# One loop over all rounds of a graph-layer kernel, with the second sums one step behind and three separate PSUM banks

## The reference, cut to what matters

```
agg = segment_sum(edge_attr, dst, 6250)        # 200000 edges x 128, dst sorted ascending
h   = relu(concat([x, agg, u[0]]) @ W1 + b1)   # 6250 x 320 @ 320 x 128
out = layernorm(x + h @ W2 + b2)               # 6250 x 128, all float32
```

## Time and profile before

| | |
|---|---|
| median of 3 runs | 278.43 us (277.78 to 278.43) |
| the profiled execution, its own time | 278.17 us |
| its span, first to last instruction | 276.3 us |
| busy: TensorE matmul, weight load | 214.3 us, 169.8 us |
| busy: VectorE, ScalarE, GpSimd | 167.3, 51.2, 41.5 us |
| moved by DMA | 110.06 MB, mean 398 GB/s |
| mean granted TensorE clock | 0.963 |

### The profile page before, as it was taken

One profiled execution on the slowest core, in us unless ns is written; L12 is line 12 of the kernel. 1 busy time (PEld: TensorE's weight loads), 2 busy tenths in 40 slices (PEclk: granted clock), 3 DMA queues, 4 the chain that ended last, 5 costly groups with the idle time before them and its releaser, 6 DMA issues.

```text
span 276.3 us, 15282 instructions
## 1 busy us (share of the span) xinstructions
PE 214.3 (78%) x6759; PEld 169.8 (61%) x6759; DVE 167.3 (61%) x426; ACT 51.2 (19%) x100; POOL 41.5 (15%) x49
## 2 busy tenths in 40 slices
PE   0998698786786796696877789895698897867872
PEld 0886577655665665575555668674577675655751
DVE  7833483774674665655773426959928768464542
ACT  0511122211211220220210211322022212121210
POOL 6400020210310300400400200300303002030020
PEclk9999999999999999999996679999899999999997
DMA  7999999999999999999999999999999999999995
GB/s 249 385 388 401 400 399 401 403 399 402 401 400 403 401 400 402 402 400 413 418 409 412 418 414 417 418 411 421 412 419 418 411 423 412 410 420 412 417 402 188
DMA packets 30911, 110.06 MB, mean 398 GB/s; under 512 B 2136, under 2 KB 3502, under 8 KB 30894
## 3 DMA queue, kind: packets, MB, share of 16 engines
q1 hardware_dynamic: 27508, 105.83, 96.1%
q10 hardware_dynamic: 3386, 4.00, 4.1%
HBM read 106.63 MB, written 3.20 MB: 397 GB/s over the span
## 4 chain that ended last, share of the span: by engine, by line
PE 62%; issue 15%; DMA 12%; DVE 6%; POOL 1%; ACT 1%; DVEq 0%; POOLq 0%; ACTq 0%
PE rows_ps L823 33%; PE cols_ps L835 15%; DMA slots<-in_edge_attr 12%; PE hid_ps L867 4%; PE hid_ps L849 3%; PE hid_ps L858 3%; PE hid_ps L843 2%; ACT rows L426 1%; DVE first_of_pair L551 1%; POOL rstd L390 1%; DVE dst_local L561 1%; DVE high L661 1%; DVE lowest L662 1%; DVE stats L641 1%; PE hid_ps L951 1%
## 5 line engine op out<-in xcount | busy, mean ns | idle before, releaser
L823 PE MATMUL rows_ps<-slots,hot 64*32 64x128 f32 x6240 | 113.2, 286 | 36.6 <-issue 32.9
L823 PEld LDWEIGHTS rows_ps<-slots,hot 64*32 64x32 f32 x6240 | 94.0, 110 | 54.2 <-issue 52.2
L619 DVE TENSOR_TENSOR agg_t<-agg_t,cols_ps 128x128 f32 (+1 forms) x65 | 21.6, 332 | 95.6 <-PE cols_ps L835 95.6
L835 PE MATMUL cols_ps<-row_hot,rows 128*128 128x128 f32 (+1 forms) x260 | 55.6, 338 | 12.2 <-ACT rows L426 6.9
L593 DVE TENSOR_TENSOR hot<-edge_node,iota 128x768 f32<-128x768 f32 x65 | 61.9, 952 | 2.7 <-issue 1.6
L426 ACT ACTIVATE rows<-rows_ps 128x256 f32<-128x256 f32 x65 | 25.0, 384 | 178.5 <-PE rows_ps L823 174.6
L835 PEld LDWEIGHTS cols_ps<-row_hot,rows 128*128 128x128 f32 x260 | 40.3, 196 | 25.9 <-issue 14.2
L390 POOL TENSOR_TENSOR rstd<-var_eps,minus_half 128x4 f32<-128x4 f32 (+1 forms) x13 | 16.6, 1276 | 202.7 <-DVE var_eps L650 202.7
L609 DVE TENSOR_TENSOR row_hot<-row_node,iota 128x256 f32<-128x256 f32 (+1 forms) x65 | 38.5, 592 | 0.0
L381 POOL TENSOR_TENSOR z<-x_rows,b_all 128x512 f32<-128x512 f32 (+1 forms) x13 | 17.2, 1321 | 26.5 <-PE hid_ps L843 26.4
L656 DVE TENSOR_SCALAR z<-z,moments,rstd (+1 forms) x49 | 16.7, 398 | 1.0 <-POOL rstd L390 1.0
(11 more groups left out here) (112 smaller groups left out, 64.6 us busy)
## 6 DMA issues: line engine op xcount, KB each, us to landing
slots<-in_edge_attr SPq DMA_DIRECT2D x65, 1536.0 KB, 17.3
x_rows<-in_x ACTq DMA_DIRECT2D x11, 256.0 KB
out<-z SPq DMA_DIRECT2D x11, 256.0 KB
dst_int<-in_dst SPq DMA_DIRECT2D x1, 384.0 KB, 3.9
dst_int<-in_dst ACTq DMA_DIRECT2D x1, 384.0 KB, 4.5
x_rows<-in_x ACTq DMA_DIRECT2D x1, 192.0 KB
out<-z SPq DMA_DIRECT2D x1, 192.0 KB
rest_slot<-in_edge_attr ACTq DMA_DIRECT2D x1, 128.0 KB, 8.8
```

Source lines behind the costliest of these rows:

```text
L619: V.tensor_tensor(cols, cols, cols_ps[:, 0:n], ALU.add).then_inc(added, 1)
L823: done = T.matmul(rows_ps[i][c * SPAN:(c + 1) * SPAN, h, 0:feats], hot[j][part, c * RUN + r, :], slots[part, j, c, r * feats:(r + 1) * fea ...
L835: done = T.matmul(cols_ps[:, 0:n], rows[i][:, h, :], row_hot[j][:, h, 0:n], start=(h == 0), stop=(h == HALVES - 1))
```

## The change

The two kinds of rounds become one (`one_lap`), with 224 columns throughout; only the very last `level2` and `add` (step 64) keep 128. The second sums run one step behind the first: `level1(t)`, then `level2(t-1)`, except that step 3's `level2` stands ahead of step 4's `level1`, and step 4's in the next round. VectorE's round runs from `add(t-1)` of the round before to `add` of step 3. `rows_ps` and `rows` have two buffers, no longer three; the two freed banks make `turn_bank` for x and `y_bank` for the second layer, so `turn_x` no longer waits for a residual, and `product2` waits for it instead. `turn_x` moves to step 1, `product1_agg` to step 1, `product2` and the (now always 512 columns wide) `product1_x` to step 2, `load_x` on ScalarE to step 3. The blocks are counted from node 128, so that the odd block with 128-row and short pieces is the first and not the twelfth; x's buffer is zeroed once (`x_zero`). The read of the counts of `judge` moves ahead of an `add`. The matmul of L916, and TensorE's wait for the plan in round 9, are gone.

TensorE:

```diff
-            def dense_lap(lap):
+            def one_lap(lap):
                 counts(lap)
                 for j in range(LAP):
                     t = lap * LAP + j
                     if j == 4:
-                        with pe.If(lap == JUDGE + 1):
-                            pe.wait_ge(plan_made, 1)
-                        with pe.If(lap > final - 1):
-                            product1_x(final, final)
-                            pe.wait_ge(rows_copied, laps * LAP)
-                            T.matmul(rows_ps[SETS[j]][:, 0, feats:512], ident[:, :], iota[:, feats:512], start=True, stop=True)
+                        level2(t - 1, j - 1, COLS)
                     level1(t, lap, j)
                     if j == 0:
-                        finished(lap)
...
+                        with pe.If(lap > 0):
+                            level2(t - 1, LAP - 1, COLS)
+                        with pe.If(lap < 1):
+                            first_products()
                     elif j == 1:
-                        product2(lap - 1, lap - 1)
+                        with pe.If(lap > 0):
+                            pe.wait_ge(added, lap * LAP + 1)
+                            product1_agg(lap - 1, start_of(lap - 1))
...
+                        level2(t - 1, j - 1, COLS)
+                        turn_x(lap, lap * 16 + x_landed(0, 0))
+                    elif j == 2:
+                        with pe.If(lap > 0):
+                            product2(lap - 1, lap - 1)
+                        level2(t - 1, j - 1, COLS)
+                        product1_x(lap, BLOCK)
                     elif j == 3:
-                        with pe.If(lap < final):
...
-                            turn_x(lap, lap, lap * 16 + 16)
-                        with pe.If(lap > final - 1):
-                            turn_x(final, final, x_landed(final))
-                    level2(t, j, True)
+                        level2(t - 1, j - 1, COLS)
...
-            with pe.Fori(0, DENSE_LAP) as lap:
-                sparse_lap(lap)
-            level2(DENSE - 1, LAP - 1, False)
-            with pe.Fori(DENSE_LAP, laps) as lap:
-                dense_lap(lap)
+            with pe.Fori(0, laps) as lap:
+                one_lap(lap)
+            level2(held, LAP - 1, DENSE_COLS)
             pe.wait_ge(added, steps + 1)
             product1_agg(final, start_of(final))
             product2(final, final)
```

VectorE:

```diff
-            def dense_lap(lap):
+            def one_lap(lap):
                 at = counts(lap)
-                for j in range(LAP):
+                for j in range(-1, LAP - 1):
                     t = lap * LAP + j
-                    add(t, at[j], True)
+                    if j == 0:
+                        with dve.If(lap == JUDGE + 1):
+                            dve.wait_ge(bad_summed, 1)
+                            dve.wait_ge(level2_done, t + 1)
+                            V.tensor_copy(bad_total[:, :], bad_ps).then_inc(bad_read, 1)
+                            dve.wait_ge(bad_read, 1)
+                    add(t, at[j + 1], COLS)
                     if j == 1:
                         residual(lap - 1, lap - 1)
...
-            with dve.Fori(DENSE_LAP, laps) as lap:
-                dense_lap(lap)
+            with dve.Fori(1, laps) as lap:
+                one_lap(lap)
+
+            add(held, 0, DENSE_COLS)
             residual(final, final)
```

Buffers, x and ScalarE's order:

```diff
-SETS = (0, 1, 0, 1, 2)
+SETS = (0, 1, 0, 1, 1)
-        rows_ps = [pb(f"rows_ps{i}", [P, HALVES, 512]) for i in range(3)]
+        rows_ps = [pb(f"rows_ps{i}", [P, HALVES, 512]) for i in range(2)]
         cols_ps = pb("cols_ps", [P, 512])
+        turn_bank = pb("turn_bank", [P, BLOCK])
         hid_ps = pb("hid_ps", [P, BLOCK])
-        y_ps = hid_ps[:, :].rearrange("p (r f) -> p r f", r=ROWS)
+        y_bank = pb("y_bank", [P, BLOCK])
+        y_ps = y_bank[:, :].rearrange("p (r f) -> p r f", r=ROWS)
...
+            G.memset(x_rows[:, :, :], 0.0).then_inc(x_zero, 1)
...
-                    if dense_lap:
+                    if t:
                         copy_rows(t)
-                    elif t + 1 < DENSE:
-                        copy_rows(t + 1)
-                    if j == 0 and lap:
-                        relu(lap - 1)
-                    elif j == 3:
+                    if j == 1:
+                        if lap:
+                            relu(lap - 1)
                         copy_x(lap)
-                    elif j == 4 and lap < final:
+                    elif j == 3 and lap < final:
                         load_x(lap + 1)
```

More of the change, by code:

```diff
@@ L90, in residual_gnn_layer, with start_of, pieces_of @@
     places = blocks + 1
[L91 to L99, removed]
+    final = places - 1
+    def start_of(i):
+        return 0 if isinstance(i, int) and i == final else FIRST + (blocks - 1) * BLOCK - i * BLOCK
+    def pieces_of(i, rows, home):
+        at = start_of(i)
+        if i == 0:
+            more = at + top_rows * P
+            mid = more + top_even
+            return ((rows[at:more, :].rearrange("(p r) f -> p (r f)", r=top_rows), home(slice(0, P), 0, top_rows)),
+                    (rows[more:mid, :], home(slice(0, top_even), top_rows, ROWS)),
+                    (rows[mid:nodes, :], home(slice(top_even, top_parts), top_rows, ROWS)))
+        if i == final:
+            return ((rows[0:FIRST, :], home(slice(0, P), 0, 1)),)
+        return ((rows[at:at + BLOCK, :].rearrange("(p r) f -> p (r f)", r=ROWS), home(slice(0, P), 0, ROWS)),)
     ctx = ExitStack()
@@ L160, in residual_gnn_layer @@
         row_hot = [sb(f"row_hot{i}", [P, HALVES, COLS]) for i in range(HOTS)]
-        rows = [sb(f"rows{i}", [P, HALVES, feats]) for i in range(3)]
+        rows = [sb(f"rows{i}", [P, HALVES, feats]) for i in range(2)]
         agg_t = sb("agg_t", [P, width])
@@ L303, in residual_gnn_layer, with x_landed @@
         pieces = places + 2
-        def x_landed(seq):
-            turns, i = seq // places, seq % places
-            return 16 * (turns * pieces + i + 1 + (2 if i >= short else 0))
+        def x_landed(turns, i):
+            return i * 16 + 16 * (turns * pieces + 3)
         @block.sync
@@ L320, in store @@
                 sp.wait_ge(normed, seq + 1)
[L321 to L328, removed]
+                for memory, home in pieces_of(i, out, lambda parts, r0, r1: z[parts, i, r0:r1, :].rearrange("p r f -> p (r f)")):
+                    sp.dma_start(memory, home).then_inc(out_stored, 16)
             sp.dma_start(dst_int[:, 0:HALVES, :], dst_pairs[0]).then_inc(dst_in, 16)
@@ L452, in relu @@
                 i = seq % places
-                m = {short: ROWS - 1, final: 1}.get(i, ROWS)
+                m = {0: top_rows}.get(i, rows_of(i))
                 act.wait_ge(hid_done, seq + 1)
@@ L691, in counts @@
                     dve.compute_val(lap + n)
[L692 to L694 removed]
+                return step_bases(lap * LAP - 1, LAP)
+            def one_lap(lap):
                 at = counts(lap)
[L696 removed]
+                for j in range(-1, LAP - 1):
                     t = lap * LAP + j
[L699 to L714 removed]
+                    if j == 0:
[5 more added lines that the diff above has]
+                    add(t, at[j + 1], COLS)
                     if j == 1:
@@ L1016, in general @@
                 pe.wait_ge(g_added, chunks * (steps + 1) + 1)
-                with pe.Fori(0, short) as i:
-                    turn_x(i + places, i, i * 16 + 16 * (pieces + 1))
-                    product1_x(i + places, i)
+                with pe.Fori(0, final) as i:
+                    turn_x(i + places, i * 16 + x_landed(1, 0))
+                    product1_x(i + places, BLOCK)
                     product1_agg(i, start_of(i))
                     product2(i + places, i)
-                for i in (short, final):
-                    turn_x(places + i, i, x_landed(places + i))
-                    product1_x(places + i, i)
-                    product1_agg(i, start_of(i))
-                    product2(places + i, i)
+                turn_x(places + final, x_landed(1, final))
+                product1_x(places + final, P)
+                product1_agg(final, start_of(final))
+                product2(places + final, final)
             with pe.If(general_if(pe) < 1):
```

162 lines of the change are left out of this document (48 added, 114 removed).

## The result

The changed kernel takes 280.34 us, median of 6 runs (279.91 to 280.98), against 278.43 for the kernel before in the same comparison: ratio 1.0078, 95% interval 1.0067 to 1.0089, **slower by 1.9 us** by the medians (2.2 by the ratio), where 1.0 was forecast. The profiled execution took 280.5 us, 2.3 above its span of 278.2.

A forecast was written before the change was run, and what follows sets the result against it. The kernel was taken as two pieces in series: 267.5 us set by transfers alone, then a tail of 8.8 us. Transfers +0 and tail +1.0 on the median of 278.43 gave 279.4 us, range 278.3 to 280.5.

The forecast's parts named there:

- The tail: Chain behind the last load, 8.8 us: the last round's new order costs +1.0 us, bounds +0.4 to +1.7.
- the 1.2 to 1.6 given: Last round, VectorE: `normalise` beside GpSimd's small addition takes 1.2 to 1.6 us, between 1.11 alone and 2.05.
- add(62): Last round, VectorE's add of step 62: expected at 267.1 us, against 262.98 before, a slip by a step.
- which leaves over 2 us a round to recover: Dense rounds: of about 4 us spare on TensorE, 1.6 go to waits, so over 2 us of lateness are recovered each round.
- recovered by round 10 or 11: After the judging in round 8: TensorE some 5 us late, well under 13, and on time again by round 10 or 11.
- the 1.6 us for waits: Late rounds, step 4: TensorE's waits for add(2) and the row copy behind ScalarE's load of x, put at 1.6 us.
- Late judging: Rival: recovery under 2 us a round leaves TensorE late in round 12; at 1 us a round 2 left, 281.4 us; chance 0.10.
- The landing: Last load's arrival, end of the transfer-bound piece: unchanged at 267.5 us, bounds -0.15 and +0.3.
- The bytes are the same: Transfer-bound piece: same bytes and descriptors, the column widths touch no transfer, so the change costs 0 there.
- Faster: Rival: without the stall at 132 us the queue stays fuller, 418 not 415.5 GB/s, landing 0.7 us earlier, 277.9 us; chance 0.08.
- It would be wrong if the landing moved by more than 0.5 us: A stated sign against the forecast: the last load no longer landing within 0.5 us of 267.5.
- The first-piece claim: Transfer-bound piece, 267.5 us: queued loads hide TensorE's lateness up to about 13 us, at no cost to transfers.

The follow-up runs named there:

- e1: The changed kernel with the judging in round 3, not 8: 278.05 us, ratio 1.001.
- e2: The changed kernel with the judging in round 10, not 8: 281.88 us, ratio 1.0148.
- e3: The changed kernel with GpSimd's addition of b2 to the next block's x put ahead of the power of this one: 278.12 us, ratio 1.0006.
- e9: The changed kernel with e3's edit and the judging in round 10: 280.44 us, ratio 1.0083.
- e11: The changed kernel with e3's edit and the judging done twice, in round 6: 279.33 us, ratio 1.0036.
- e6: The changed kernel with `variance` directly behind `residual` and `normalise` a step earlier: 295.49 us, ratio 1.0583.
- e8: The changed kernel with the edits of e1, e3 and e6; in the last round 128 columns for product1_x and the second sums and adds of steps 62, 63: 280.96 us.
- e12: e8 without e6's edit: 278.29 us, ratio 1.0003.

## Why the prediction was off

**The tail.** Forecast +1.0 for the last round's order. Measured +0.9 in e1, where nothing else is late, and 5.84 us behind the last add for 5.85. `normalise` took 1.24 us beside GpSimd's 0.46, within the 1.2 to 1.6 given. This part was right in mechanism and size. That add(62) came at 268.07 and not near 267 is the lateness, not the order.

**The step that failed** is "which leaves over 2 us a round to recover", and with it "recovered by round 10 or 11". The size of the lateness was about right: some 5 us were forecast, and step 44 was 6.0 late. But TensorE got back 0.5 to 0.9 us a round, and was 3.3 late at step 64. I summed TensorE's own work (15.4 us), added 1.6 for waits that I saw, and compared it with 19.5. What I didn't do is follow one late round through all engines to where it closes on itself: `add`, `variance`, power, addition, load of x, `turn_x`, `add`, 18.7 us. The change leaves three steps between asking for x and turning it, where there were four, and I took the load for hidden; but behind full DMA engines it takes 6.9 us. e2, e3 and e9 show the ring: with x's load no longer behind `variance` the late round takes 17.9 us and not 19.0. Even 17.9 is more than my 17.0 (15.4 + 1.6), so the 1.6 us for waits were too few as well; what makes up that rest was not followed. The slow recovery left +2.4 us. The rival "Late judging" was this, with 2 us left by its own count; it had 0.10, and should have had most.

**The landing** was forecast unchanged, bounds -0.15 to +0.3; it was -1.3. "The bytes are the same" left out instruction code, which is the likely cause. The rival "Faster" had the earlier landing (0.7 us), by a higher rate that didn't come: 417 GB/s for 416.

**Sum**: -1.3 + 0.9 + 2.4 = +2.0 against +1.91 in the last add and +1.9 in the medians. The two errors have opposite signs, and it is luck that the time still fell inside the range of 278.3 to 280.5. "It would be wrong if the landing moved by more than 0.5 us" was met.

The first-piece claim that TensorE's lateness costs no transfer below 13 us held as far as this kernel went: at 6.0 us late, 10.6 us of depth, the stretch moved 417 GB/s. As a bound it was too wide: in e11, 11.6 us of lateness, with first sums 1.2 us longer at the lower clock, already cost 1.8 us of landing.

## What to carry to other kernels

A queue of loads hides a late engine only if the engine can catch up before the last load; sum the round in its late form, along the ring through every engine and every small load in it, not the engine's own work. Place one-off work early, where rounds to recover are left (2.3 us here for one constant). And a small load that is asked for while the queue is full is slow, here 6.8 to 6.9 us from issue to use: ask for it as soon as its buffer's last reader can be made to finish.

## What the runs showed of the hardware

- A load's landing and the bytes moved are two measures: landings 1.3 us apart at totals within 0.3 us of transfer. Code fetches of 16 KB hold one of 16 engines for 1.1 us; the kernel before had five between 137 and 181 us, four at the start of its second loop and one some 23 us later.
- The sixteen engines finish their shares of one load up to 3 us apart, and the last one sets the landing: at 181.3 for 181.7, when the other fifteen were done by 179.7.
- Loads of x of 256 KB, issued at 216.4 and 235.0 on ScalarE's queue, were used 6.8 and 6.9 us later, one of 64 KB issued at 253.7 also 6.9 us later, while 1.5 MB edge loads issued within 2 us of them took 13.0 to 15.0 us.
- Loads that took 9.0 us or more from issue to landing kept 416 GB/s; where the next load was issued 1.2 us ahead of the last one's landing, 30 us moved 381.
- TensorE behind a wait of 4.9 us ran its first sums in 2.81 us, the next in 1.85, and then in 1.59 again; in e6, with a wait each round, the mean granted clock was 0.907 against 0.973 in the changed kernel.
- TensorE's sequencer can come 1.7 to 1.9 us late to the end of a program whose last product was long done (e8, e12).
